# Retention and the last attention stage in one block: the last stage's buffers over retention's freed ones, its weights split inside retention's slots, its first rows turned between the last output projections

## The reference

```python
h = ssm_kernel(x, ...)                                # (16, 192, 512): first stage
h = h + retention(layernorm(h), Wq, Wk, Wv, Wg, Wo)   # 8 heads, causal, decayed; o * rms * g_norm * silu(g), then @ Wo
h = h + ffn(layernorm(h), W_gate, W_qkv)              # last stage:
#   gating = softmax(x @ W_gate.T); one head of 16 is chosen for each row
#   k_shared, v_shared = the chosen head's k, v (v weighted by the gate)
#   y = softmax(causal(q k_shared^T / sqrt(32))) v_shared, for all 16 query heads
```

## Time and profile before

| | |
|---|---|
| three runs | 1356.54, 1358.33, 1358.59 us (median 1358.33) |
| the profiled execution | 1354.94 us, of which span 1353.2 us |
| PE busy | 1235.0 us, 91% |
| DVE, ACT, POOL busy | 54%, 41%, 38% |
| mean granted TensorE clock | 0.966 |
| slice 26 of 40 (846 to 880 us) | PE 4 tenths busy, the slices on either side 9 and 8 |

### The profile page before, as it was taken

One profiled execution on the slowest core, in us unless ns is written; L12 is line 12 of the kernel. 1 busy time (PEld: TensorE's weight loads), 2 busy tenths in 40 slices (PEclk: granted clock), 3 DMA queues, 4 the chain that ended last, 5 costly groups with the idle time before them and its releaser, 6 DMA issues. The chain is left out here.

```text
span 1353.2 us, 23060 instructions
## 1 busy us (share of the span) xinstructions
PE 1235.0 (91%) x8280; PEld 1021.5 (75%) x8280; DVE 724.5 (54%) x1357; ACT 560.7 (41%) x1769; POOL 520.0 (38%) x721
## 2 busy tenths in 40 slices
PE   0489999999999997799999999488999999999997
PEld 0378888888888886587877777377788887888875
DVE  7685666556665531545455454144554655545444
ACT  3444433344444222433333322123555555555546
POOL 2766766676666720422332332011213212132122
PEclk9989999999999998799999998788999999999999
DMA  4133222322222228656566511333413315233141
GB/s 161 62 109 117 94 105 98 117 88 115 102 102 109 94 107 289 192 160 187 165 187 187 156 41 47 136 85 87 110 50 94 95 48 141 54 90 87 32 118 33
DMA packets 81792, 150.60 MB, mean 111 GB/s; under 512 B 11664, under 2 KB 44560, under 8 KB 80144
## 3 DMA queue, kind: packets, MB, share of 16 engines
q1 hardware_dynamic: 81680, 149.15, 35.5%
HBM read 67.19 MB, written 56.62 MB: 91 GB/s over the span
## 5 line engine op out<-in xcount | busy, mean ns | idle before, releaser
L1579 ACT ACTIVATE probs<-psum,row_max 128x128 f32<-128x128 f32 (+1 forms) x384 | 143.2, 389 | 40.1 <-DVE row_max L1735 26.3
L988 ACT ACTIVATE square_scratch<-psum 128x128 f32<-128x128 f32 x192 | 50.9, 275 | 181.6 <-PE psum L1195 181.6
L1735 DVE TENSOR_REDUCE row_max<-psum 128x2 f32<-128x384 f32 (+1 forms) x128 | 79.2, 619 | 77.2 <-PE psum L1960 42.3
L1868 POOL TENSOR_TENSOR h_rows<-h_rows,y_normed 128x512 f32<-128x512 f32 x24 | 30.8, 1281 | 223.5 <-DVE y_normed L1752 223.5
L1845 POOL TENSOR_TENSOR picked_rows<-picked_rows 128x768 f32<-128x768 f32 (+1 forms) x64 | 61.2, 956 | 96.5 <-DVE picked_rows L1717 92.8
L1139 POOL TENSOR_TENSOR rr<-ss,consts_r 128x3 f32<-128x3 f32 x64 | 14.4, 224 | 205.1 <-ACT square_scratch L988 205.1
L710 PE MATMUL psum<-m,basis 128*128 128x64 f32 x384 | 48.9, 284 | 43.4 <-POOL basis L662 43.4
L681 POOL TENSOR_TENSOR stage<-stage 128x512 f32<-128x512 f32 x48 | 81.6, 1722 | 14.5 <-DVE stage L563 14.5
L1743 DVE COPY raw_f<-psum 128x512 f32<-128x512 f32 x64 | 44.2, 691 | 77.9 <-PE psum L1973 77.8
L1924 PE MATMUL psum<-wf_high,x_high 128*128 128x512 f32 x192 | 81.8, 426 | 3.6 <-DVE q_t_low L1708 2.5
L710 PEld LDWEIGHTS psum<-m,basis 128*128 128x128 f32 x384 | 49.6, 203 | 45.3 <-issue 43.3
(11 more groups left out here) (255 smaller groups left out, 3614.6 us busy)
## 6 DMA issues: line engine op xcount, KB each, us to landing
qk<-stage SPq DMA_DIRECT2D x24, 512.0 KB, 2.6
v<-stage SPq DMA_DIRECT2D x24, 512.0 KB, 2.6
g<-gate_rows SPq DMA_DIRECT2D x24, 512.0 KB, 2.7
q_stack_t<-q_t_high SPq DMA_DIRECT2D x128, 96.0 KB, 2.3
q_stack_t<-q_t_low SPq DMA_DIRECT2D x128, 96.0 KB, 2.2
qk_rows<-qk SPq DMA_DIRECT2D x16, 512.0 KB, 6.1
stage<-in_w_r SPq DMA_DIRECT2D x6, 1024.0 KB, 5.1
h_tok<-h_rows SPq DMA_DIRECT2D x24, 256.0 KB, 2.0
```

The source lines that it names most:

```text
L988: last = nc.scalar.activation(sqs[:, h % 2, t], psum[:, OB[h % 2], t * RV:(t + 1) * RV], ACT.Square, accum_out=ss[:, h % 2, t:t + 1])
L1579: last = nc.scalar.activation(pr[:, g % 2, c], psum[:, SB[g % 3], c], ACT.Exp, bias=mx[:, g % 3, x:x + 1], accum_out=dsum[:, t, h:h + 1])
L1735: V.reduce_max(mx[:, g % 3, 0:nh], psum[:, SB[g % 3], 0:nh * w].rearrange("p (h n) -> p h n", h=nh), AX, negate=True).then_inc(s_max.sem, 1)
```

## The change

The block boundary between retention and the last stage goes. `stage_f`'s code is cut in pieces (a dictionary `f` for each engine) that `stage_q` calls at places of its own, and a rest, `run`, behind it. Five things follow:

1. Buffers: the last stage's tensors are laid over retention's in an order such that each lies over one that is free by then. Four waits (`ended`) guard what is not free yet; `load_h` of pairs 0 to 3 waits for the last values and the last transposes of pair 6.
2. Weights: the three 1 MB weights of the last stage are loaded at the end of slots 1, 2 and 3. Two are split inside slots 2 and 3 (ScalarE one copy, VectorE two halves), in the order k, q; the third (v) waits in `raw_f` and is split between the q parts. There is one raw buffer in place of two.
3. The gate weight and the constants come in slots 1 and 2; row statistics of pair 0 in slot 7, its scales on GpSimd behind head 5 of pair 7.
4. The ninth slot is a function `last`: x transposes of pair 0 between the last three y transposes, logits behind the first projected tile, `q_proj(0, 0)` behind the second. PSUM banks of pair 0 are other ones (`xt_bank`, `lg_bank`, `q_bank`, `k_bank`, `v_bank`).
5. In `run`, the projections of pair 0 go on without the waits for a bank's reader where another bank is used; `logits(1)` stands between `scores(0)` and `scores(1)`.

The diff, cut to its core (that `here` goes from every slot, since the ninth slot is gone, is left out):

```diff
@@ stage_q, sync @@
+            else:
+                for n in range(2):
+                    sp.wait_ge(pv_sum.sem, pv_sum.at(i - 1, RH))
+                    f["rows"](n)
             if i + 2 < PAIRS:
                 load_qk(sp, i + 2, 0)
             if back:
...
+            else:
+                for n in range(2, 4):
+                    sp.wait_ge(yt_sum.sem, yt_sum.at(i - 1, 2 * NT))
+                    f["rows"](n)
...
             if back:
                 store(i - 1, 1)
                 store(i - 1, 2)
+            if i == 1:
+                f["constants"]()
+            if i in (1, 2, 3):
+                f["weight"](i - 1)
@@ stage_q, scalar @@
+                if i == 2 and t == 1:
+                    f["gate_weight"]()
+                if i in (2, 3) and t == 1:
+                    f["weight"](i - 2)
...
         pairs(slot)
-
-    def vector(dve):
+        f["norm"](0, 0)
+        f["norm"](0, 1)
+        f["x_split"](0, 0)
+        y_split(PAIRS - 1, 0, 1)
+        f["norm"](0, 2)
+        y_split(PAIRS - 1, 1, 1)
+        f["x_split"](0, 1)
+        y_split(PAIRS - 1, 2, 1)
+        f["x_split"](0, 2)
+
+    def vector(dve, f):
@@ stage_q, vector @@
                 if back:
                     add_h(i - 1, m - 1)
                 elif m < HG - 1:
                     split_weights(m - 1)
...
+                if i == 2 and m == 2:
+                    f["gate_weight"]()
+                if i in (2, 3) and m > 1:
+                    f["weight"](i - 2, m - 2)
+                if not ahead and m == 1:
+                    f["row_stats"](0)
...
         pairs(slot)
-
-    def gpsimd(pool):
+        gate_o(PAIRS - 1, RH - 1)
+        f["x_split"](0, 0)
+        y_split(PAIRS - 1, 0, 1)
+        y_split(PAIRS - 1, 1, 1)
+        f["x_split"](0, 1)
+        y_split(PAIRS - 1, 2, 1)
+        f["x_split"](0, 2)
+        f["row_stats"](1)
+        add_h(PAIRS - 1, 0)
+        f["choose"](0)
+        add_h(PAIRS - 1, 1)
+        f["q_split"](0, 0)
+        add_h(PAIRS - 1, 2)
+
+    def gpsimd(pool, f):
@@ stage_q, tensor @@
+        def last():
+
+            i = PAIRS - 1
+            f["x_transposes"](0, 0)
+            pe.wait_ge(y_low.sem, y_low.at(i, 2))
+            y_transposes(i, 0, 1)
+            pe.wait_ge(y_low.sem, y_low.at(i, 3))
+            y_transposes(i, 1, 1)
+            f["x_transposes"](0, 1)
+            pe.wait_ge(y_low.sem, y_low.at(i, 4))
+            y_transposes(i, 2, 1)
+            f["x_transposes"](0, 2)
+            wo(i, 0, 0)
+            wo(i, 0, 1)
+            f["logits"](0)
+            wo(i, 1, 0)
+            wo(i, 1, 1)
+            f["q_proj"](0, 0)
+            wo(i, 2, 0)
+            wo(i, 2, 1)
@@ stage_f, vector @@
+        def run():
+            q_split(0, 1)
+            weight(2, 0)
+            q_split(0, 2)
+            weight(2, 1)
+            q_split(0, 3)
+            gate(0)
...
@@ stage_f, tensor @@
+        def run():
+            q_proj(0, 1)
+            pe.wait_ge(q_low.sem, q_low.at(0, 1))
+            q_proj(0, 2)
+            ended["added"](pe)
+            q_proj(0, 3)
+            kv_proj(0, WK, 0, ALL)
+            pe.wait_ge(q_low.sem, q_low.at(0, 3))
+            kv_proj(0, WK, 1, ALL)
+            pe.wait_ge(q_low.sem, q_low.at(0, 4))
+            kv_proj(0, WK, 2, ALL)
+            pe.wait_ge(k_picked.sem, k_picked.at(0, 2))
+            pe.wait_ge(w_low, 6)
+            kv_proj(0, WV, 0, ALL)
+            x_transposes(1, 0)
...
+            pe.wait_ge(v_picked.sem, v_picked.at(0, 2))
+            scores(0)
+            pe.wait_ge(kt_out.sem, kt_out.at(0, 1))
+            logits(1)
+            scores(1)
```

More of the change, by code:

```diff
@@ L869, in pairs @@
     def pairs(slot):
-        for i in range(PAIRS + 1):
-            slot(i, i < PAIRS, i > 0, i + 1 < PAIRS)
+        for i in range(PAIRS):
+            slot(i, i > 0, i + 1 < PAIRS)
     def rows(sp, name, i, t, dst, s):
@@ L932, in store, with slot @@
                     sp.dma_start(h2[P:T, 2 * i + b], hin[b * R:(b + 1) * R, t]).then_inc(stored[t].sem, 16)
-        def slot(i, here, back, ahead):
+        def slot(i, back, ahead):
             if ahead:
@@ L966, in sync, with scalar @@
         for t in range(NT):
-            sp.wait_ge(stored[t].sem, stored[t].at(PAIRS - 1, 1))
-    def scalar(act):
+            load_h(PAIRS - 1, t)
+        for t in range(NT):
+            store(PAIRS - 1, t)
+    def scalar(act, f):
         for s in (qkt_out, squares, y_high):
@@ L1091, in split_weights, with slot @@
                                    ALU.mult, ALU.subtract).then_inc(w_low, 1)
-        def slot(i, here, back, ahead):
-            if here:
-                masked(i, 0)
+        def slot(i, back, ahead):
+            masked(i, 0)
             if back:
                 gate_o(i - 1, RH - 1)
-            if here:
-                masked(i, 1)
+            masked(i, 1)
             if back:
                 y_split(i - 1, 0, 1)
-            if here:
-                gate_o(i, 0)
+            gate_o(i, 0)
             if back:
@@ L1221, in wo, with slot @@
                 last.then_inc(wo_sum.sem, 1)
-        def slot(i, here, back, ahead):
-            if here:
-                scores(i, 0)
+        def slot(i, back, ahead):
+            scores(i, 0)
             if ahead:
@@ L1242, in slot @@
                 y_transposes(i - 1, 0, 1)
[L1243 to L1244 removed]
+            values(i, 1)
             if back:
@@ L1529, in sync, with constants @@
-        store(PAIRS - 1, 2)
-        for i in range(PAIRS - NH, PAIRS):
-            sp.wait_ge(stored[i % NH].sem, stored[i % NH].at(i // NH, 1))
+        def constants():
+            sp.dma_start(gw_raw[:, :, :].rearrange("p k n -> p (k n)"), d["w_gate"]).then_inc(const_in, 16)
+            sp.dma_start(desc[:, :], d["consts_f"]).then_inc(const_in, 16)
+            sp.dma_start(maskb[:, :], d["mask_f"]).then_inc(const_in, 16)
+            sp.dma_start(identb[:, :], d["ident_b"]).then_inc(const_in, 16)
@@ new lines, in weight, with rest @@
+        def weight(n):
+            if n:
+                sp.wait_ge(w_low, 2 * n)
+            sp.dma_start(raw[:, :, :], d["w_f"][2 + ORDER[n]]).then_inc(w_in[n], 16)
+        def run():
+            q_stack(0)
+            v_swap(0)
+            rest()
+        def rest():
+            for i in range(PAIRS):
+                if i:
+                    store(i - 1, 2)
+                    if i + 3 == PAIRS - 1:
+                        ended["stored"](sp)
+                    if i + 3 < PAIRS:
+                        load_h(i + 3)
+                if i + 1 < PAIRS:
+                    q_stack(i + 1)
+                store(i, 0)
+                store(i, 1)
+                if i + 1 < PAIRS:
+                    v_swap(i + 1)
+            store(PAIRS - 1, 2)
+            for i in range(PAIRS - NH, PAIRS):
+                sp.wait_ge(stored[i % NH].sem, stored[i % NH].at(i // NH, 1))
@@ L1533, in scalar @@
+        return {"constants": constants, "weight": weight, "rows": load_h, "run": run}
     def scalar(act):
@@ L2141, in stage_f @@
+        return {"x_transposes": x_transposes, "logits": logits, "q_proj": q_proj, "run": run}
     return Stage(sync, scalar, vector, gpsimd, tensor)
@@ L2162, in _ @@
                 units.sync(sp, prefetch)
-                retention.sync(sp)
+                f = attention.sync(sp)
+                retention.sync(sp, f)
+                f["run"]()
             @block.scalar
@@ L2167, in _ @@
                 units.scalar(act)
-                retention.scalar(act)
+                f = attention.scalar(act)
+                retention.scalar(act, f)
+                f["run"]()
             @block.vector
@@ L2172, in _ @@
                 units.vector(dve)
-                retention.vector(dve)
+                f = attention.vector(dve)
+                retention.vector(dve, f)
+                f["run"]()
             @block.gpsimd
@@ L2177, in _ @@
                 units.gpsimd(pool)
-                retention.gpsimd(pool)
+                f = attention.gpsimd(pool)
+                retention.gpsimd(pool, f)
+                f["run"]()
             @block.tensor
```

474 lines of the change are left out of this document (213 added, 261 removed).

## The result

| | before | changed |
|---|---|---|
| runs beside the first comparison | 1356.54 to 1361.13 us, median 1358.46 | 1323.82 to 1326.51 us, median 1326.05 |
| ratio, 95% interval | | 0.9758 (0.9743 to 0.9774) |
| span of the profiled execution | 1353.2 us | 1323.5 us |
| mean granted TensorE clock | 0.966 | 0.980 |
| the same kernel timed again, four runs | median 1357.87 (nine runs) | 1327.51 to 1329.88 us, median 1328.5, ratio 0.9785 (0.9772 to 0.9799) |

Faster by 2.2 to 2.4%, 29 to 32 us. The forecast was 1332, range 1325 to 1340. Both medians lie in the range; the first lies under the forecast's own part of it, 1328 to 1337. Two medians of one kernel differ by 2.4 us; the experiments show where that can lie, and leave open why.

A forecast was written before the change was run, and what follows sets the result against it. TensorE was taken to bound both stages, so time was winnable at the seam: -27.5 there, +1.0 clock behind, +0.5 retention, -26.0 in all. Profiled execution 1328.9, median 1332 us; own range 1328 to 1337, with rivals' near ends 1325 to 1340.

The forecast's parts named there:

- the seam: Between retention and the last stage: `scores(0)` starts at 895.3 instead of 922.77, a gain of 27.5 us.
- the stack: At the seam: q's 32 transfers on SyncE end last, 23.25 us from first issue to `scores(0)`; TensorE done some 6 us earlier.
- The start of `wo`: Twelve transposes ahead of the last 72 `wo` matmuls delay their start by 1.0 us, bounds 0 and 3.0.
- The first six at the lower clock: First six of the last 72 `wo` matmuls take 2.70 us in place of 1.4: +1.2, range 0 to 1.2.
- The sum of 31.7 us: TensorE's work from the old first of the last 72 `wo`, 838.69, to q's last sum, forecast at 870.4.
- The halves of v's split: On VectorE between the q splits: two 1.15 us halves make q's last low part 0.3 us later.
- The clock behind S: From `scores(0)` on, low TensorE clock after the stack wait slows two more score groups: +1.0 us, bounds 0 to 2.5.
- Retention: Slots 2 to 4: h rows land later behind weight loads, bounds 0 and 3 us each; 0.5 us in all.
- A: Rival at the seam: the stack doesn't end last, TensorE reaches `scores(0)` at 889; gain 33 to 34, 1325 us; chance 0.09.
- B: Rival in retention: late h rows and weight halves holding up GpSimd cost 5 to 10 us, 1337 to 1342; chance 0.10.
- D: Rival: merge only moves the seam's chain, e.g. slot 7 waits for h rows; gain 18 to 22, 1338 us; chance 0.06.
- C: Rival in the last stage's 128 steps: operands in other places cost 0.20 us each, cancelling 26 us, or more; chance 0.03.

The follow-up runs named there:

- two_queues: Changed kernel with pair 0's 16 low-part q stack transfers issued on ScalarE's queue, the 16 high-part ones staying on SyncE; 1319.65 us.
- same_again: The changed kernel unaltered, timed once more; median 1328.50 us.
- v_split_late: Changed kernel with VectorE's two halves of the v weight's split moved behind the last low part of q; 1328.82 us.
- logits_mixed_all: Changed kernel with narrow logits matmuls laid between wide ones, at the seam and in the steps, logits(1) staying in a row; 1323.65 us.
- no_mixing: Changed kernel with the last y transposes and 72 `wo` matmuls unmixed; x transposes, logits and first q part follow behind; 1338.01 us.
- rows_late: no_mixing with h rows of pairs 0 to 3 issued behind the last store, their statistics behind the last `add_h`; 1352.18 us.
- two_queues_12: Changed kernel with 12 of pair 0's stack transfers on ScalarE, 20 on SyncE starting at the last high part, v's split late; 1315.79 us.
- loads_behind: Changed kernel with constants and three weights issued one slot later, behind the h rows and ahead of the gate rows; 1328.41 us.
- copy_1mb: Changed kernel with one extra, unread 1 MB DRAM-to-DRAM transfer issued on SyncE at the end of slots 1 to 6; 1333.32 us.
- all_together: Changed kernel with two_queues_12, loads_behind and logits of pairs 1 to 7 mixed in twos behind the first q part's matmuls; 1310.56 us.

## Why the prediction was right, and where its terms were off

**What it rested on held.** The gain was to come from the seam alone, the stack was to be the last wait with TensorE done some 6 us earlier (6.52), no gap over 4 us was to be left before q, the stack to take 23.25 us (23.1), the tail from the last sum of q to the last low part 1.6 us (867.40 to 868.91: 1.5), the steps to stay as they are. Each row says so. Two_queues shows that the stack was the last wait: issued faster, it lets S come 5.1 us sooner.

**The terms that were off** are all between V and the last sum of q, and on one side. The start of `wo` was to be 1.0 us late; it is 0.4 early (V to first `wo` 6.89 us, before 7.28). The first six at the lower clock, +1.2: absent. Logits took 2.6 (2.7), the dip behind them 1.6 (1.7), and 48 `q_proj` 8.4 (8.4). The sum of 31.7 us counts from the old first `wo`, 838.69; measured from there, q was summed at 867.40, after 28.7 us, 3.0 sooner than forecast, and S came 3.3 sooner (892.04 against 895.3).

In this profile the clock stayed up where it had fallen before: eight y transposes took 1.06 us, not 1.94, with the x transposes of 834.10 standing in what was a wait of 2.71 us. I had 3.0 us as the bound above for twelve transposes at the lower level and nothing below zero, though the same sentence said that they might end the low clock. That they keep the clock up is not shown, and part of this miss is luck. Ten profiles have them there. In four (changed, same_again, v_split_late, logits_mixed_all) the 24th `wo` ends 12.6 us behind V. In the other six the clock fell among the transposes and the 24th `wo` ends 13.1 to 13.7 behind V, as in two_queues:

```profile
838.10 1.01 PE L2009 MATMUL psum<-ident,x 128*128 128x128 f32 x4
...
840.15 1.06 PE L2009 MATMUL psum<-ident,x 128*128 128x128 f32 x4
840.87 0.78 PE L1257 MATMUL psum<-wo_high,y_high 128*128 128x512 f32 x1
```

In the three where that wait is bare it ends 14.4 (before), 13.1 (no_mixing) and 13.5 (rows_late) behind V. So the twelve transposes cost nothing there, and the order of the work alone doesn't fix where the clock falls.

**The halves of v's split**, +0.3: nothing to be seen, since the SyncE queue's first 16 issues took up the earlier start (v_split_late).

**The clock behind S**, +1.0, bounds 0 to 2.5: 1.1 in the first profile (431.5 against 430.4), 4.1 in the second, over my bound. The term was right in its place and too narrow: the dips behind the rows of logits fall differently in different executions, and I had priced only the two score groups. Between the two profiles of this program this, and not retention, makes the difference (V 831.17 and 831.29); its other six executions have no profile here. Its reason was too simple as well: two_queues had the low clock behind S without the long wait.

**Retention**, +0.5: it paid nothing, 249.96 us from the first `wo` to V against 249.99. But the slack was as thin as worked out: h was forecast to land at 628.2 in slot 2 and landed at 627.5; in slots 3 and 4, forecast just in time, no wait shows.

**Conversion.** The spans differ by 29.7 us, the first medians by 32.4, the second by 29.4. The forecast of 26.0 missed by 3.7 in the spans: 3.3 in S (0.24 of them already at V), 0.5 that retention didn't pay, and 0.1 the other way behind S. The median was missed by more, 1332.3 against 1326.05. In the profiled executions 1328.9 was forecast and 1326.51 came, 2.4 less. The other 3.9 are the step from a profiled execution to a median: the old one lay 3.4 us under its median, the new one 0.5 over. So the first median fell below the forecast's own range and into the part that was added for A, which did not come about; the second, 1328.50, lies just inside. That both lie between 1325 and 1340 owes something to luck.

**The rivals.** A (TensorE last) didn't come about by itself; two_queues_12 makes it true, and S then comes at 886.2. B (retention pays) is refuted for the median by loads_behind; GpSimd held up by the weight halves, had it reached TensorE, would show from the first `wo` to V, which hasn't grown. B is priced: with 1 MB more in front it begins (copy_1mb), with 3 MB it costs 53 to 55 us. D is out: slot 7 has no wait for h. C: S to the end is 431 to 434 us in every kernel with the rows of logits, before 430.4; with them mixed 428.3, with no long wait ahead as well 422.8. So operands in other places cost nothing that could be seen.

## What to carry to other kernels

Before merging two stages, split the gap between them by what each of its parts waits for: here early rows and statistics gave 15.5 of 30.5 us, more than the merged block with early weights (6.4), and mixing the two stages' work 8.6, some 2 of them by TensorE's clock. Twelve transposes, the first four in a bare wait of 2.7 us, cost nothing that could be seen; count on that, not on more. When many small transfers are the last wait, look at the issues as well as at the bytes (here 0.66 us for each, at a DMA share of 0.60), and give another idle engine a share that ends before its own next work. The row of 24 narrow matmuls was best laid between wide ones in the steps, and not at the seam, where it covered another engine's return. The other seam of this kernel, into retention, is untouched: from 520 to 580 us TensorE is busy 40.9 of 60 us in the changed kernel.

## What was not expected of the hardware

- TensorE's granted clock fell with the engine busy without a pause: behind rows of 24 matmuls of 32 and 16 columns, 2.6 us long, to the lower level for some 3 us (0.72 over 954 to 960), a loss of some 1.8 us each time, in some pairs and not in others. The rows ahead of the prediction had shown one such fall, behind steady logits, and the prediction used it; that it goes with the order of the matmuls was new. The same matmuls in twos between wide ones never showed it in the steps (logits_mixed_all, all_together). The Trainium skill (TensorE: Matmul & The Clock Gate, "HAM oscillation") tells of idle gaps as what throttles; here a row without gaps did it too.
- The same program behaved in two ways behind S, 431.5 and 434.5 us, so that two medians of four differed by 2.4 us.
- 32 transfers of 96 KB within SBUF took 21.2 us to issue from one queue (148 GB/s, DMA share 0.60) and 14.6 from two (215 GB/s, share 0.83; 0.88 to 0.91 us for each issue on either queue, in place of 0.66).
- A start of that queue 0.37 us earlier changed nothing 11 us later.
